# Attention probabilities turned by VectorE block transposes and a DRAM round trip, six batches in flight, a new order table

## The reference, cut to what matters

```python
def _mha(x, kv, Wq, Wk, Wv, mask, causal):      # attentions 0 and 1
    energy = jnp.einsum('bhsk,bhtk->bhst', Q, K)
    lengths = jnp.sum(energy[:, :, 0, :] != 0, axis=-1)
    energy = jnp.where(cols[None, None, None, :] >= lengths[:, :, None, None], -jnp.inf, energy)
    ...
    score = jax.nn.softmax(energy / jnp.sqrt(dk), axis=-1)
    out = jnp.einsum('bhst,bhtk->bhsk', score, V) * m
```

## Time and profile before

| | |
|---|---|
| median of 3 runs | 4001.53 us (3999.12 to 4001.73) |
| span of the profiled execution | 3996.0 us |
| TensorE busy | 3939.4 us, 44820 matmuls |
| VectorE busy | 2932.9 us |
| ScalarE busy | 2676.8 us |
| GpSimd busy | 1233.8 us |
| DMA | 69.65 MB, mean 17 GB/s |

### The profile page before, as it was taken

How to read it: one execution, slowest core, us unless ns; L and a number is a source line. 1 busy time by engine, 2 the same in 40 slices (tenths; PEclk the granted TensorE clock), 3 DMA queues, 4 the chain that set the end, 5 groups by cost and what they waited for, 6 DMA issues and landing times.

```text
span 3996.0 us, 116007 instructions
## 1 busy us (share of the span) xinstructions
PE 3939.4 (99%) x44820; PEld 3452.9 (86%) x44820; DVE 2932.9 (73%) x10721; ACT 2676.8 (67%) x8449; POOL 1233.8 (31%) x2247
## 2 busy tenths in 40 slices
PE   7999999999999999999999999999999999999998
PEld 7888888888888888888888888888888888888886
DVE  4677777777777777777777777777777777777764
ACT  3676766776766766767767767667667667676663
POOL 1233333233232332333332332323323333323321
PEclk9999999999999999999999999999999999999999
DMA  3000000000000000000000000000000000000000
GB/s 146 5 15 18 10 18 18 10 18 17 10 18 17 10 18 16 12 18 10 18 18 10 17 18 10 18 18 10 18 17 11 18 10 18 18 10 18 18 3 5
DMA packets 66498, 69.65 MB, mean 17 GB/s; under 512 B 7456, under 2 KB 64800, under 8 KB 65056
## 3 DMA queue, kind: packets, MB, share of 16 engines
q1 hardware_dynamic: 65952, 62.25, 5.0%
HBM read 53.83 MB, written 8.39 MB: 16 GB/s over the span
## 4 chain that ended last, share of the span: by engine, by line
PE 89%; DVE 6%; ACT 2%; issue 1%; POOL 1%; DMA 0%; SPq 0%; DVEq 0%; POOLq 0%; ACTq 0%
PE gen_ps L513 54%; PE gen_ps L505 16%; PE gen_ps L635 6%; PE scores_ps L609 5%; PE gen_ps L647 3%; PE scores_ps L595 3%; PE scores_ps L602 2%; PE scores_ps L588 1%; ACT oT L747 1%; DVE wide L935 1%; DVE zn L980 1%; DVE v L1040 1%; DVE rdenm L977 1%; DVE res L1044 1%; DVE plainT L1043 1%
## 5 line engine op out<-in xcount | busy, mean ns | idle before, releaser
L513 PE MATMUL gen_ps<-actT,w_sb 128*128 128x128 f32 x10752 | 1345.7, 278 | 12.2 <-DMA w_sb<-weights_dram 8.3
L513 PEld LDWEIGHTS gen_ps<-actT,w_sb 128*128 128x128 f32 x10752 | 1261.4, 192 | 67.6 <-issue 47.4
L836 POOL TENSOR_TENSOR rstd<-ve,consts 128x1 f32<-128x1 f32 x448 | 283.4, 633 | 1421.7 <-DVE ve L987 842.1
L747 ACT ACTIVATE probT<-gen_ps 128x512 f32<-128x512 f32 x1024 | 577.2, 634 | 210.5 <-PE gen_ps L505 207.3
L781 ACT ACTIVATE prob<-scores_ps,negmax 128x128 f32<-128x128 f32 x2048 | 568.6, 417 | 199.0 <-DVE negmax L1025 198.9
L505 PE MATMUL gen_ps<-consts,prob 128*128 128x128 f32 x4096 | 598.3, 276 | 11.4 <-ACT prob L781 5.7
L505 PEld LDWEIGHTS gen_ps<-consts,prob 128*128 128x128 f32 x4096 | 467.4, 141 | 122.1 <-ACT prob L781 57.2
L513 PE MATMUL gen_ps<-w_sb,wide 128*128 128x256 f32 x2056 | 465.4, 379 | 0.9 <-DVE wide L1165 0.6
L513 PE MATMUL gen_ps<-w_sb,actT 128*128 128x256 f32 x1792 | 462.5, 381 | 2.7 <-ACT actT L747 2.1
L897 POOL TENSOR_SCALAR prob<-prob,rden 128x128 f32<-128x128 f32 x1024 | 366.7, 380 | 314.7 <-DVE rden L1098 314.7
L747 ACT ACTIVATE actT<-gen_ps 128x256 f32<-128x256 f32 (+1 forms) x512 | 238.8, 466 | 285.0 <-PE gen_ps L505 284.9
(11 more groups left out here) (118 smaller groups left out, 6085.0 us busy)
## 6 DMA issues: line engine op xcount, KB each, us to landing
actT<-xT_dram SPq DMA_DIRECT2D x64, 128.0 KB, 2.2
ctx_rms<-x_dram SPq DMA_DIRECT2D x64, 128.0 KB, 2.2
ctx<-ctx_dram SPq DMA_DIRECT2D x64, 128.0 KB, 2.2
ctxT<-ctxT_dram SPq DMA_DIRECT2D x64, 128.0 KB, 2.3
mask<-mask_dram SPq DMA_DIRECT2D x128, 64.0 KB, 2.1
out_dram<-res SPq DMA_DIRECT2D x64, 128.0 KB, 1.7
w_sb<-weights_dram SPq DMA_DIRECT2D x2, 2048.0 KB, 18.8
w_sb<-weights_dram SPq DMA_DIRECT2D x2, 1024.0 KB, 20.5
```

The source lines that it names most:

```text
L513: last = nc.tensor.matmul(ps, lhsT(c), rhs(c), start=(c == 0), stop=(c == chunks - 1))
L747: release(nc.scalar.activation(dst, take(act, name, b)[:, 0:width], ACT.Copy), name, b)
L836: nc.gpsimd.tensor_tensor(dst, src, const("expo")[:, 0:width], ALU.pow)\
```

## The change

- The TensorE `turn` is gone, and with it the ScalarE copy. VectorE instead executes one block transpose for each unit (`nc.vector.transpose` of 128x512, each block of 32x32 by itself, read from `prob` with a stride of 4 elements) into a new buffer `turned` (N_T = 4 units). SP then sends the unit to a DRAM tensor (256 KB as 128 rows of 2 KB; `send`) and reads it back into `probT` with the blocks in their transposed places (512 pieces of 512 bytes; `fetch`). A fetch waits for the landing of its send; `values` and `out2` wait for the landing of the fetches. `probT` holds two attentions (N_PT = 2).
- Six batches in flight (G = 6) instead of four; buffers that are short-lived get depths of their own (wide 2, ctxT and mask3 3, qT 3 and apart from `wide`, plainT 4, v16 4, pen 4). Banks of `gen_ps` are handed out by planned release times, and a bank can have two readers.
- Moved from VectorE to ScalarE: the two masked copies of the queries for a < 2 (L935, now two activations), the copy of the values `v64` (L1040), the scalings L1144 (`rms_norm`) and L1175 (`norm_x4`; VectorE computes a 128x1 product `nb4` for it).
- Moved from VectorE to GpSimd: the addition of epsilon (L987, L1111, L1114, L1139). `rsqrt` on GpSimd becomes an addition, a wait for it, and the power, nine times a batch.
- SP's queue has an order of its own from the table: 37 steps a batch.
- `BESIDE` is gone: no identity matmuls. PERIOD is 57.420651 instead of 69.731652, and all times in the table are new.

```diff
-G = 4
+G = 6
+N_WIDE = 2
+N_CTXT = 3
+N_Q = 3
+N_V = 4
+N_K = 4
+N_PT = 2
+N_T = 4
+N_FAR = 4
-PERIOD = 69.731652
+PERIOD = 57.420651
...
-            def turn(a, b, u):
-                N = unit(a, b, u)
...
-                transposes(f"t{a}{u}", b, [prob[:, N % 4, k, :] for k in range(HU)])
...
             def values(a, b):
...
-                        read_out(pe, f"t{a}{u}", b)
+                        fetched(pe, a, b, u)
...
-                elif name == "turn":
-                    probT_read(act, a, b)
-                    copy_out(f"t{a}{u}", b, flat(probT[:, u, :, :]), 512)
...
+            def turn(a, b, u):
+                n = turned_unit(a, b, u)
+                if a == 2:
+                    dve.wait_ge(sem("normed"), U * b + u + 1)
+                else:
+                    dve.wait_ge(sem("exp_done"), unit(a, b, u) + 1)
+                if n >= N_T:
+                    dve.wait_ge(sent_sem(n), 16 * (n // N_T))
+                nc.vector.transpose(turned[:, n % N_T, :, :, :].rearrange("p t k j -> p k t j"),
+                                    prob[:, u, :, :].rearrange("p k (i t) -> p k t i", t=R)).then_inc(sem("turned"), 1)
...
+                def send(a, b, u):
+                    n = turned_unit(a, b, u)
+                    k = T_OF[a, b]
+                    sp.wait_ge(sem("turned"), n + 1)
+                    if k >= N_FAR:
+                        fetched(sp, *TURNED[k - N_FAR], u)
+                    sp.dma_start(turned_d[n % (U * N_FAR)].rearrange("q (i t) x -> (q i) (t x)", t=R),
+                                 turned[:, n % N_T, :, :, :].rearrange("p t k j -> p (t k j)"))\
+                        .then_inc(sent_sem(n), 16)
+                def take_back(a, b, u):
+                    n = turned_unit(a, b, u)
+                    sp.wait_ge(sent_sem(n), 16 * (n // N_T + 1))
+                    probT_read(sp, a, b)
+                    sp.dma_start(probT[:, TURN_OF[a, b] % N_PT, u, :, :],
+                                 turned_d[n % (U * N_FAR)].rearrange("q t x -> t q x")).then_inc(fetched_sem(a, b, u), 16)
...
-            def rsqrt(src, dst, wait, signal, b, width=1):
+            def rsqrt(src, dst, eps, wait, signal, b):
                 pool.wait_ge(sem(wait), b + 1)
-                nc.gpsimd.tensor_tensor(dst, src, const("expo")[:, 0:width], ALU.pow)\
-                    .then_inc(sem(signal), 1)
+                nc.gpsimd.tensor_scalar(dst, src, eps, 0.0, ALU.add, ALU.add).then_inc(sem("padded"), 1)
+                padded[0] += 1
+                pool.wait_ge(sem("padded"), padded[0])
+                nc.gpsimd.tensor_tensor(dst, dst, const("expo")[:, 0:1], ALU.pow).then_inc(sem(signal), 1)
...
-                    for c in range(C):
-                        ins = nc.vector.scalar_tensor_tensor(
...
+                elif name == "queries":
+                    ps = take(act, f"m{a}", b)[:, 0:D].rearrange("p (c s) -> p c s", c=C)
+                    first_read(act, f"m{a}", b)
+                    q_free(act, a, b)
+                    for e in range(2):
+                        ins = nc.scalar.activation(qT[:, Q_PLACE[a, b] % N_Q, :, e, :], ps, ACT.Copy,
+                                                   scale=const("parityq")[:, e:e + 1])
+                    release(ins, f"m{a}", b)
```

727 lines of the change are left out of this document (406 added, 321 removed).

## The result

The changed kernel takes 4627.3 us (median of four runs, 4622.2 to 4633.75) against 4001.3 us (3999.12 to 4001.73) before: the ratio is 1.157, with a 95% interval of 1.155 to 1.158. The forecast was 3772 us, with a range of 3520 to 4010. It was wrong in sign and by 855 us.

What follows compares the result with a forecast made beforehand. TensorE bounds the kernel now; after the change VectorE (53.4 us) and TensorE (52.9) wait for each other, 56.5 us a period. 64 x 56.5 + 150 = 3766, plus 5.5 for the median: 3772 us, range 3520 to 4010.

Steps and rivals of the forecast that it cites:

- TensorE's own period, 52.9 us: TensorE without the turns and a wait for ScalarE: 60.75 - 7.0 - 0.8 = 52.9 us a period.
- One unit's turn, 0.62 us from start to start: VectorE's 128x512 block transpose, priced at 0.62 us, between 435 ns and 1.15 us: 16 make 9.9 us a period.
- third rival: Costly transpose: 1.15 us each on VectorE, which alone sets a period of 64.5 us, 4284 us total; chance 0.10.
- The rest of VectorE's list: VectorE's need of 47.4 us less 3.9 moved away, before 9.9 for transposes: 53.4 us in all, busy 51 to 53.
- The way through DRAM, 6.4 us (bound 9): One unit's send and fetch through SP and DMA: 6.4 us, 5.5 to 9, covered before values0, values1 and values4.
- second rival: Longer way: landings through DRAM take 1.3 us more both ways, 58.7 us a period, 3917 us total; chance 0.19.
- The walk of the order, 56.0 + 0.5 us: One period walked from the end of scores2 closes after 56.0 us; 0.5 added for uncounted semaphores gives 56.5.
- The granted clock: TensorE's clock stays 1.00 in the steady stretch; under 0.97 would show the prediction wrong.
- fourth rival: Lower TensorE clock for a third of its 52 us: 14 us more, 70 us a period, about 4640 us; chance 0.04.
- GpSimd: the price: Nine rsqrt a batch gain an addition of 0.4 us and a 0.1 wait: 4.5 us more, about 24 a period.
- up to 2 us: VectorE's period: about four waits for rstd in the layernorms grow by 0.5 us each, up to 2 us.
- Start and end, 150 us: Span outside the 64 steady periods: 108 us now, forecast 150 us in all, bounds 100 and 210.

Runs made afterwards that it cites:

- e8: e4 plus 42 idle identity products a batch ahead of three TensorE waits: 4177.0 us, 62.80 us a period.
- e16: Changed kernel without sends and fetches, transposes writing straight to probT and reading whole runs of 32 columns: 3955.4 us, 59.41 us a period.
- e3: Changed kernel without sends and fetches, the transpose writing straight to probT: 4264.8 us, 64.38 us a period.
- e7: Changed kernel, but after two batches only a quarter of each unit is sent to DRAM while the fetch brings all: 4488.3 us.
- e6: Changed kernel with three SyncE table entries moved, so all sends of attentions 0, 1 and 2 precede their first fetch: 4466.2 us.
- e17: e16 plus 20 idle products ahead of TensorE's waits and GpSimd's reciprocal root in one instruction: 3883.7 us, 58.30 us a period.
- e14: e6 plus 20 idle products ahead of three TensorE waits, whole computation kept: 4361.8 us, 65.30 us a period.
- e10: e4 with GpSimd's reciprocal root in one instruction instead of two, the small constant left out: 4043.0 us.
- e4: Changed kernel without sends and fetches, and with a maximum of the unit with itself replacing each transpose: 4077.7 us, 61.47 us a period.
- e13: e4 with GpSimd's scaling of attention 2's probabilities 16 columns wide instead of 128: 4023.2 us.
- e1: Kernel before plus 36 VectorE operations ahead of its first batch, six each of six forms of transpose, copy and maximum: period 60.75 us.
- e5: Changed kernel with transposes reading whole runs of 32 columns instead of every fourth column: 4432.1 us, 66.51 us a period.
- e2: Changed kernel with each transpose replaced by a maximum of the unit with itself, way through DRAM kept: 4499.7 us.
- e12: e6 with transposes reading whole runs and each fetch split into four 64 KB transfers that put the keys right: 6764.6 us.
- e9: e4 plus 20 idle products a batch ahead of three TensorE waits: 4009.8 us, 60.30 us a period.

## Why the prediction was wrong, step by step

**TensorE's own period, 52.9 us: right at a clock of 1.00.** e8 gives 52.8. In the changed kernel TensorE is busy 422.27 of 500 us, 58.9 a period: the same work takes some 6 us more at the lower clock.

**One unit's turn, 0.62 us from start to start: wrong, about 1.03 (1.10 by itself).** The step failed where the forecast chose between bounds of 0.44 and 1.15 us. It took the nearest row by shape (128x512), and that row is a good price for a transpose that reads in order: 0.60 to 0.63 us from start to start in e16. The change reads every fourth column. The forecast named that stride as what spoke for its third rival, gave the rival 0.10, and dismissed it with operations none of which was a transpose with a stride. The stride is worth 69.7 - 66.5 = 3.2 us a period in the changed kernel and 5.0 (e3 to e16) without the way through DRAM; the 16 x 0.41 = 6.6 us that it adds to VectorE's list came through in part only, where the rival had counted such time one to one. The rest of VectorE's list was priced about right: it is busy 50.6 us a period in e16 (425.65 of 500 us), the forecast had 51 to 53.

**The way through DRAM, 6.4 us (bound 9), and which ways are covered: wrong, 9.6 (values3) to 14.0 (values1).** The packets were priced well: the forecast's share of the DMA engines was 0.50 to 0.70, its list had 0.45 to 0.65, and it is 0.43. Two things were missed. On the path a send takes mostly 3.0 to 4.5 us and a fetch 3.4 to 5.5 (chain from 1000 to 1600 us), above the medians of 2.4 and 3.5 and the forecast's 2.5 and 3.0; that the transfers of one attention hold each other up is what e7 speaks for, not more. And SyncE's order holds a ready send behind a fetch's wait, in attention 1 above all, whose way the walk had called covered. The forecast had seen the reverse of this (send2.2 ahead of fetch2.0) and walked it with a send that lands in 2.5 us. It had put the point at which the gain is gone at 10 us. Without the way, the period is 5.3 us shorter (e3); moving three entries gives 2.8 (e6). In its second rival the forecast's own terms give 56.5 + 2.6 = 59.1 us a period, not 58.7.

**The walk of the order, 56.0 + 0.5 us: wrong by 2 to 3 us.** With both causes gone, and transposes at the forecast's own price, e16 needs 59.4 us. TensorE is busy 54.1 of them, and its waits between 1000 and 2000 us (total us, times, longest) are these:

```profile
PE scores_ps L650 <- POOL plainT L968: 42.5, 17, 2.8
PE gen_ps L571 <- ACT actT L887: 20.6, 17, 1.4
PE gen_ps L563 <- ACT zn L861: 19.2, 17, 1.2
```

That is 2.5, 1.2 and 1.1 us a period, for GpSimd before scores2 and twice for ScalarE. The walk had none of the three; the waits that it had (out2 1.5, values3 0.6, scores1 1.1) don't appear. So its 3 us of waits had about the right size for another reason than the one given. The clock and the root are worth 1.1 us of the difference (e17); as far as these rows show, the last 1.8 lie in these waits, but no run takes them away one by one: with 4.8 us of idle products e17's TensorE is busy 494 of 500 us, near its bound of 57.6.

**The granted clock: wrong.** 0.92, below the 0.97 that the forecast's own list set as the mark. Its fourth rival was right in kind and much too dear: it had 14 us a period for the clock, and filling three of the waits gave 1.6 us in e14. That its time, 4640 us at 70 us a period, is the closest of all to the measured 4627 at 69.7 is luck: most of the loss is the way through DRAM and the stride. The forecast's sum had no term for the clock in the steady state.

**GpSimd: the price was too high, the place wrong.** The added instruction takes 0.225 us, not 0.4, and the power behind it 0.562 instead of 0.633. The forecast's "up to 2 us" stands in its sum only as far as the walk's 2.6 us of VectorE's waits hold it; taking the instruction out gives 0.5 us a period (e10). Where GpSimd does hold the period up is before scores2, 2.5 us of TensorE's wait. The scalings of attention 2 are a tie in e4 (1.3 us less gave 0.8, e13); in the changed kernel VectorE waits for them 0.6 us in all.

**Start and end, 150 us: right to 19 us.** Without the way through DRAM it is 137 to 156 us, with it 169 to 188.

In sum, a period: 69.7 - 56.5 = 13.2 us, of which by removing one after the other the way through DRAM takes 5.3 (e3), the stride 5.0 (e16), clock and root 1.1 (e17), and 1.8 stay with waits of the new order that no run takes apart. The order matters: the same stride alone was worth 3.2.

What the forecast called rivals were not alternatives. The costly transpose (4284 us) and the longer way (3917) both came true, and each was priced alone. But even both together come to 3772 + 512 + 145 = 4429 us by the forecast's prices; the other 200 us are a way through DRAM that was longer than in the second rival and lay where the walk had seen cover, the clock, and the waits for GpSimd and ScalarE.

## What to carry to other kernels

An operation that the trace doesn't show is priced by the row that shares its access pattern, not only its shape; where none does, the dear bound deserves more than the 0.10 that it got here, where one stride made 0.4 us sixteen times a batch. A round trip through a shared in-order queue is priced by walking the queue with the landings under load, transfers of the same burst included, and where the order allows it, sends go ahead of the first wait for a landing. A walk of one period has to close: the wait in front of the step where it begins is as likely as any other. When several independent terms are uncertain in the same direction, the bad case is their sum, and an experiment's stand-in operation needs its own check, since here it slowed another engine.

## What the runs showed of the hardware

- A VectorE block transpose of 128x512 takes 0.71 us in fp32 and bf16 alike when it reads in order (e1), 0.70 in fp32 when it reads whole runs of 32 (e5), and 1.09 to 1.10 with every fourth element; a copy with the same steps takes 0.61 (e1). From start to start it is 0.60 to 0.63 and 0.99 to 1.04. One square of 128x128 takes 0.311 us, the figure that the Trainium skill gives for bf16 (VectorE: DVE Perf Modes, The three transpose paths); the trace agrees, and shows that four squares in one instruction don't cost four times as much.
- A maximum on VectorE with two SBUF inputs slows GpSimd beside it: a scaling of 128x128 from at most 0.54 us to up to 1.33 (means 0.39 and 0.48), a 128x512 product from 1.28 to 1.71 (the changed kernel and e2). A transpose of the same length doesn't (e5).
- GpSimd's scaling of 16 columns has a median of 0.28 us (e13), of 128 columns 0.376 (e4): about three quarters of it don't depend on the width. The means, 0.395 and 0.48, hold the slowing by the maximum.
- SyncE needs 0.42 us to issue a 256 KB fetch (changed kernel) and 0.71 for one of 64 KB with another order of addresses (e12; medians).
- The granted clock of the steady state rose from 0.97 to 1.00 when 20 idle products filled part of TensorE's waits (e9), and from 0.93 (e6) to 0.99 with the way through DRAM in place (e14). The products of scores2 went from 365 (e4) and 371 ns (e6) to 276 in both.
